# Head attention: the sum over heads by four accumulating transposes, its logarithm turned back by a fifth

## The reference

```python
q, k, v = (x @ W.T + b).reshape(B, S, 16, 16)      # each with its own W and b
scores = einsum("bqnd,bknd->bnqk", q, k) / sqrt(16)
attn = softmax(scores, axis=1)                     # over the 16 heads, not over the keys
out = einsum("bnqk,bknd->bqnd", attn, v).reshape(B, S, 256) @ Wo.T + bo
x = layernorm(x + out)
```

## Time and profile before

| what | value |
|---|---|
| median of three runs | 4204.99 us |
| profiled execution | 4201.35 us, of which the span is 4199.6 |
| mean granted TensorE clock over the span | 0.988 |
| PE, PEld busy over the span | 3943.1 us (94%), 3290.3 us (78%) |
| DVE, ACT, POOL busy over the span | 3122.2, 2889.5, 2173.2 us |
| the head attention | from the start to about 1,450 us |

### The profile page before, as it was taken

The page is one execution under the profiler, slowest core; times in us unless marked ns, Lnnn a source line. Parts: engine busy times, 40 slices in busy tenths (PEclk is TensorE's granted clock), DMA queues, the critical chain, the costliest instruction groups (busy, mean ns, idle before and its releaser), DMA issues.

```text
span 4199.6 us, 95669 instructions
## 1 busy us (share of the span) xinstructions
PE 3943.1 (94%) x36004; PEld 3290.3 (78%) x36064; DVE 3122.2 (74%) x7348; ACT 2889.5 (69%) x7337; POOL 2173.2 (52%) x2168
## 2 busy tenths in 40 slices
PE   5999999999999769999999999999999999999997
PEld 3777777777777658888888888888888888888886
DVE  3999999999999856666666666666777777777775
ACT  3666666666666557777777777767777777777775
POOL 3999999999999823333333333332333333333332
PEclk8999999999999989999999999999999999999999
DMA  5454444543445010000000000010000000000000
GB/s 106 67 76 64 62 69 70 78 65 57 72 70 70 14 63 12 20 17 17 19 17 14 17 21 16 17 32 10 26 23 22 27 22 22 23 26 25 20 24 25
DMA packets 175104, 159.25 MB, mean 38 GB/s; under 512 B 22194, under 2 KB 173620, under 8 KB 174644
## 3 DMA queue, kind: packets, MB, share of 16 engines
q1 hardware_dynamic: 174644, 153.13, 19.7%
HBM read 52.40 MB, written 25.17 MB: 18 GB/s over the span
## 4 chain that ended last, share of the span: by engine, by line
PE 40%; ACT 11%; issue 8%; DVE 3%; POOL 3%; SPq 0%; DMA 0%; POOLq 0%; DVEq 0%; ACTq 0%
PE b_X L1434 11%; PE b_F L1503 5%; PE b_M L1556 5%; PE b_S L1454 4%; PE b_F L1582 4%; PE b_S L1464 3%; PE b_M L1475 3%; ACT L1162 2%; PE b_M L1547 2%; ACT L1168 2%; ACT b_hn L1077 1%; ACT b_g L1162 1%; ACT b_PT L1200 1%; DVE b_qT L1235 1%; DVE b_kT L1235 1%
## 5 line engine op out<-in xcount | busy, mean ns | idle before, releaser
L352 ACT ACTIVATE a_p<-a_S 128x512 f32<-128x512 f32 x1024 | 528.8, 603 | 273.9 <-PE a_S L523 273.9
L399 DVE TENSOR_REDUCE a_half_max<-a_S 128x128 f32<-128x1024 f32 x512 | 602.7, 1219 | 143.4 <-PE a_S L513 137.3
L252 POOL TENSOR_TENSOR a_z<-a_p 128x1024 f32<-128x1024 f32 x256 | 604.9, 2363 | 152.5 <-ACT a_p L352 152.5
L1434 PE MATMUL b_X<-b_wqkv,b_hT 128*128 128x512 f32 x2304 | 649.0, 417 | 1.3 <-DVE b_hT L1270 1.3
L1503 PE MATMUL b_F<-b_hnT,b_w 128*128 128x256 f32 (+1 forms) x4224 | 585.3, 287 | 5.8 <-issue 5.8
L1194 ACT ACTIVATE b_p<-b_S,b_nb 128x256 f32<-128x256 f32 (+1 forms) x1024 | 444.6, 446 | 178.4 <-DVE b_nb L1246 178.2
L1503 PEld LDWEIGHTS b_F<-b_hnT,b_w 128*128 128x128 f32 (+1 forms) x4224 | 533.3, 187 | 18.6 <-issue 6.2
L1434 PEld LDWEIGHTS b_X<-b_wqkv,b_hT 128*128 128x128 f32 x2304 | 417.0, 190 | 100.0 <-issue 21.8
L971 POOL TENSOR_TENSOR b_t<-b_t 128x512 f32<-128x512 f32 x128 | 165.8, 1295 | 554.1 <-DVE b_t L1218 554.1
L416 DVE TENSOR_TENSOR a_p<-a_p,a_O 128x1536 f32<-128x1536 f32 x256 | 445.9, 1742 | 3.1 <-ACT a_O L326 3.1
L1246 DVE CUSTOM_DVE_ANT_0 b_S<-b_S,b_mask,b_rn 128x256 f32<-128x256 f32 (+1 forms) x1024 | 399.5, 450 | 1.2 <-PE b_S L1454 1.2
(11 more groups left out here) (153 smaller groups left out, 8651.1 us busy)
## 6 DMA issues: line engine op xcount, KB each, us to landing
a_q<-a_parts SPq DMA_DIRECT2D x256, 128.0 KB, 5.1
a_k<-a_parts SPq DMA_DIRECT2D x256, 128.0 KB, 5.1
a_x<-in_x SPq DMA_DIRECT2D x16, 512.0 KB, 4.0
a_xr<-in_x SPq DMA_DIRECT2D x64, 128.0 KB, 5.2
x_after_heads<-a_n SPq DMA_DIRECT2D x64, 128.0 KB, 5.3
b_x<-x_after_heads SPq DMA_DIRECT2D x16, 512.0 KB, 4.1
x_after_layer<-b_xo SPq DMA_DIRECT2D x32, 256.0 KB, 2.3
b_x<-x_after_layer SPq DMA_DIRECT2D x16, 512.0 KB, 4.2
```

Of the source, the lines that this page charges most:

```text
L252: nc.gpsimd.tensor_tensor(z8[:], e[:, 0:8], e[:, 8:16], ALU.add).then_inc(s_zt, 1)
L352: nc.scalar.activation(probs[u % NE][:, hs], S[:, hs], ACT.Exp, scale=HDIM ** -0.5).then_inc(s_exp, 1)
L399: nc.vector.tensor_reduce(out=half_max[:, half], in_=S[:, 8 * half:8 * half + 8].rearrange("p h q -> p q h"), axis=AX.X, op=ALU.max, negat ...
L1434: last = nc.tensor.matmul(X[i][:], hT_of(k, a), wqkv[:, b, k, i * INNER:(i + 1) * INNER], start=(k == 0 and (a, b) == PART_PAIRS[0]), stop ...
```

## The change

Four things change.

1. `sum_z`: the four products take the partial sum as the weights and the identity as the moving operand, and are transposes (`is_transpose`). They still accumulate in `Z`, which now holds the sum transposed.
2. A new function `turn_back` transposes the logarithm once more, into `LN_Z`, the rest of the bank `YZ`. Both inverses are computed by ACT from `LN_Z`, one after the other (`inverses`), in the place where only `zinv_to_psum` stood.
3. On PE the order behind the scores is now: parts 0 to 2 of `times_v`, `output` where there is one, `turn_back`, part 3 of `times_v`, `less_part` for part 0.
4. Waits: `ln_of_z` and `sum_z` wait for the new semaphore or for `s_zp` in place of `s_zp` or `s_lz`, and DVE waits for `s_zp` ahead of the residual sum.

```diff
-    Z = YZ[:, 1, :P]
+    Z, LN_Z = YZ[:, 1, :P], YZ[:, 1, P:]
...
         def ln_of_z(n, u):
             U = UNITS * n + u
             act.wait_ge(s_z, U + 1)
-            need(act, s_zp, U)
+            need(act, s_lb, U)
             nc.scalar.activation(ln_z[:], Z, ACT.Ln, scale=1.0 / Z_SCALE).then_inc(s_lz, 1)
-            act.wait_ge(s_lz, U + 1)
+
+        def inverses(n, u):
+
+            U = UNITS * n + u
+            act.wait_ge(s_lb, U + 1)
             need(act, s_pp, U - 1)
-            nc.scalar.activation(zinv[u % 2][:], ln_z[:], ACT.Exp, scale=-1.0).then_inc(s_zi, 1)
-
-        def zinv_to_psum(n, u):
-
-            U = UNITS * n + u
+            nc.scalar.activation(zinv[u % 2][:], LN_Z, ACT.Exp, scale=-1.0).then_inc(s_zi, 1)
             need(act, s_av, U)
-            nc.scalar.activation(ZI, ln_z[:], ACT.Exp, scale=-1.0).then_inc(s_zp, 1)
+            nc.scalar.activation(ZI, LN_Z, ACT.Exp, scale=-1.0).then_inc(s_zp, 1)
...
-                    zinv_to_psum(nn, uu)
+                    inverses(nn, uu)
...
+                    dve.wait_ge(s_zp, UNITS * nn + uu + 1 if exists(nn) else UNITS * SEQS)
                     dve.wait_ge(s_Y, TILES * nr + qt + 1)
...
             if pair == 0:
-                need(pe, s_lz, U)
+                need(pe, s_zp, U)
                 pe.wait_ge(s_zt, 2 * U + 2)
             for j in (2 * pair, 2 * pair + 1):
-                last = nc.tensor.matmul(Z, ident[:], z4[uu % 4][:, j], start=(j == 0), stop=(j == 3),
-                                        skip_group_check=True)
+                last = nc.tensor.matmul(Z, z4[uu % 4][:, j], ident[:], start=(j == 0), stop=(j == 3),
+                                        is_transpose=True, skip_group_check=True)
...
+        def turn_back(n, u):
+
+            U = UNITS * n + u
+            pe.wait_ge(s_lz, U + 1)
+            nc.tensor.transpose(LN_Z, ln_z[:], ident[:]).then_inc(s_lb, 1)
...
-                    for part in range(4):
+                    for part in range(3):
                         times_v(nn, uu, par if not back else 1 - par, part)
+                nz, _, uz = lagged(n, u, 2, UNITS)
+                no, _, uo = lagged(n, u, 4, UNITS)
+                if uo % TILES == TILES - 1 and exists(no):
+                    pe.wait_ge(s_lz, UNITS * nz + uz + 1 if exists(nz) else UNITS * SEQS)
+                    output(no, uo)
+                if exists(nz):
+                    turn_back(nz, uz)
+                if exists(nn):
+                    times_v(nn, uu, par if not back else 1 - par, 3)
                 for i, part in lesses:
                     if part == 0:
                         less_part(n + 1, i, part)
-                nz, _, uz = lagged(n, u, 2, UNITS)
-                nn, _, uu = lagged(n, u, 4, UNITS)
-                if uu % TILES == TILES - 1 and exists(nn):
-                    pe.wait_ge(s_lz, UNITS * nz + uz + 1 if exists(nz) else UNITS * SEQS)
-                    output(nn, uu)
```

More of the change, by code:

```diff
@@ L122, in head_attention @@
     s_lz = sem("ln_z")
+    s_lb = sem("ln_z_turned_back")
     s_zi = sem("zinv")
```

## The result

The changed kernel takes 4256.45 us (4251.99 to 4261.28, four runs) against 4202.44 of the kernel before beside it: a ratio of 1.0128, with a 95% interval of 1.011 to 1.0147. It is 54 us slower. The forecast was 4267, and slower with a chance of 0.90.

A forecast was written before the change was run, and what follows sets the result against it. The prediction took a loop of POOL's first adding, `negmax`, L523 and four exps as the bound. Losses of 1.58 + 2.55 = 4.13 us a sequence, 66 us over 16, on 4201.35 gave 4267; range 4218 to 4305.

The forecast's parts named there:

- What bounds: Head attention: POOL's first adding, `negmax`, the maximum-subtracting products and four exps set the unit, 5.38 of 5.42 us.
- the loop: Head attention: the chain from POOL's first adding through `negmax`, L523 and four exps back to POOL, 5.38 us.
- room: PE's free time before L523 needs the array: about 0.34 us in unit 6, 0.24 in unit 4, none in 12 and 14.
- The sum over heads at nothing: PE's sum over heads: halving its passes frees about 0.45 us a unit, but waits for exps absorb it; gain nothing.
- The fifth transpose in the cut, 0.45: PE inside `times_v`: weight-width changes delay following work 0.45 us; uncovered in six units, 1.58 us a sequence.
- The output ahead of the transpose, 2.55: Units 3, 7, 11, 15: inverses wait behind `output`, so exps start 0.54 to 0.69 us late; 2.55 us a sequence.
- the 0.36 that the prediction had for L523 alone: Unit 7: lateness of the maximum-subtracting products on PE taken alone, 0.36 us, beside 0.69 for the exps.
- The wait on DVE: Unit after an output: the residual waits for ZI, 0.62 us later, hidden beside exps 0.69 late; no cost.
- The clock: Rival on PE: more transposes drop the clock to 1.2 GHz, over 1,300 us more; chance 0.01.
- low bound: Cut `times_v` costing only 0.11 us, a transpose in stream without draining: 1.3 us a sequence, 21 in all, 4223.
- the 4223: Whole-kernel time in us if the cut in `times_v` is cheap (0.11 us); this rival had chance 0.15.

The follow-up runs named there:

- E6: Kernel before with POOL's first adding of heads split into two pairs after the third exponential and six after the fourth: 4180.36 us, ratio 0.9935.
- E8: Kernel before with POOL's first adding of heads split 2 and 6, but left whole in unit 8: 4160.73 us, ratio 0.9893.
- E1: Kernel before with only the sum over heads made accumulating transposes, nothing turned back: 4205.09 us, ratio 1.0002.
- E5: Changed kernel with ACT's last evacuation of q or k and those of V ahead of the two inverses: 4244.34 us, ratio 1.0093.
- E7: Kernel before with POOL's first adding of heads in two equal instructions, the first already after the second exponential: 4316.33 us, ratio 1.026.
- E2: Kernel before plus one transpose that nobody reads, between the third and fourth part of the products with V: 4237.08 us, ratio 1.0084.
- E3: Kernel before plus one transpose that nobody reads, behind the fourth part of the products with V: 4217.69 us, ratio 1.0036.

## Why the prediction was right

*What bounds.* Right. `negmax` still ends 0.15 behind L253 in the kernel after (median 0.148 over the stage), E6 to E8 move the time by moving that end, and E1 shows that the sum over heads isn't in the loop. Units 12 and 14 are the exception, where PE's products for V end last; the prediction had no room there, and the table agrees. The Trainium skill (Trainium Architecture — The Big Picture, What this means for kernel authors) says that of the engines only DVE and GpSimd contend for a port of SBUF, by an exclusive lock. By that rule `negmax`, which reads two tiles of SBUF, waits for a whole POOL addition, and the traces agree: it ends 0.15 behind (median 0.147 of 202 before, 0.148 of 195 after). So what was said of the engines at the start, that they meet only through semaphores, is too strong: `negmax` waits for no semaphore of POOL.

*The sum over heads at nothing.* Right: 1.0002.

*The fifth transpose in the cut, 0.45.* The mechanism was right, the size a little too large: the transpose took 0.33 and not 0.39, since the weights that weren't loaded ahead cost 0.05 and not the 0.11 that I took from L523. That makes 0.39, and the table shows it bare in units 12 and 14. It was taken six times in the sum, beside the room: 1.21 us a sequence measured where 1.58 was forecast. Of the idle of about 0.2 on both sides, 0.20 stands ahead of the transpose and 0.12 behind it.

*The output ahead of the transpose, 2.55.* Right in place and order, with 2.18 measured. In unit 7 ZI starts 5.33 us after the unit's first exp (741.48 less 736.15), exactly as worked out (716.75 less 711.42). What was too large stands behind it, on ACT: the next evacuation starts 0.17 after ZI and not 0.22, which is the 0.05 of unit 7; in unit 15 the two L300 free ACT 0.53 after their start and not 0.57; and in units 3 and 11 L311 starts 0.29 after ZI, where the forecast had 0.22 and another 0.2 of waiting for L479: 0.54 and not 0.66. E5 shows the part of ACT's queue in units 7 and 15, and leaves in unit 7 the 0.36 that the prediction had for L523 alone.

*The wait on DVE.* Right: in unit 7 the residual starts 6.28 us after L525's start (741.77 less 735.49), where it was 5.65 (716.47 less 710.82), so 0.63 later, forecast 0.62, hidden by the exps' delay. E5 takes part of that delay away and gains 0.28 in unit 7, as far as PE lets it; unit 8, where DVE would be late, loses nothing there either.

*The clock.* Full as before, with 80 transposes more a sequence. The rule of the Trainium skill about transposes and the clock gate (TensorE: Matmul & The Clock Gate, Part 4: PE-mode transpose) decided nothing here; whether it holds was not tried, since matmuls stay in every unit.

The forecast was 66 us of loss, and 54 were measured; the 12 between them are these two sizes, 0.37 us a sequence each, and 0.03 in the other units. One sum of the prediction is a little off: its low bound adds up to 2 x 0.11 + 2.55 - 4 x 0.34 = 1.41 us a sequence and not 1.3, which leaves the 4223 in place within 1 us. Not tried: the changed kernel with the output behind the turning back, since output and logarithm share a bank of PSUM, and it would have needed another wait.

## What to carry to other kernels

Before work is taken off the engine that looks busiest, look for the instruction right behind that work and ask what else it waits for: here each half of the sum stood in front of two score banks, of which the second starts 0.05 us after the exponential that frees it, and half of that work less bought 0.5 us of waiting. A step that turns a result back through an engine adds its place in that engine's order and in the next one's queue; this place, not its own 0.3 us, was the price. And an instruction that has no semaphore in common with another can still be bound to its end, so read the ends of both engines side by side.

## What the runs showed of the hardware

- A DVE instruction with two operands in SBUF, of 0.30 us, lasts up to 1.35 (E6) when a POOL addition runs, and ends about 0.15 after it. So starting POOL 1 us earlier made the kernel 2.6% slower (E7). DVE's product with ZI, which has one operand in PSUM (L416), ran beside the same additions and took 1.74 in all of 202 cases.
- A full-width transpose between two groups of 32-column products costs PE 0.39 us (E2), and behind them 0.15 where a full-width L477 follows (units 3 and 11 of E3) but 0.25 where weights of three rows follow (units 12 and 14). The Trainium skill (TensorEngine Tiling (Array Packing), Key Properties) says that a change of the tiling mode drains TensorE; the traces agree, with 0.10 to 0.27 us of idle before the first load of each group of 32-column weights and of what follows it, where loads of one group that wait for nothing follow each other within 0.05.
- A transpose of f32 with accumulation takes the same 0.11 us in stream, from start to start, as one pass of an f32 product (L557 after, L555 before).
